# A graph network's gathers and one-hots: rolled loops with a bounds check against an unrolled program with its counts in PSUM

## The reference

```python
def _cheb_norm(src, dst, n):
    deg = jax.ops.segment_sum(jnp.ones((src.shape[0],), jnp.float32), src, num_segments=n)
    dinv = jnp.where(deg > 0, jax.lax.rsqrt(jnp.maximum(deg, 1.0)), 0.0)
    return -dinv[src] * dinv[dst]
def _cheb_conv(x, src, dst, norm, W0, W1, b):
    def prop(h):
        return jax.ops.segment_sum(h[src] * norm[:, None], dst, num_segments=x.shape[0])
    return x @ W0 + prop(x) @ W1 + b
h = _cheb_conv(x, src, dst, norm, W1_0, W1_1, b1)
h = _layer_norm(h, gamma, beta)
h = jnp.where(h >= 0, h, 0.01 * h)
out = _cheb_conv(h, src, dst, norm, W2_0, W2_1, b2)
return _layernorm(x + out)
```

## Time and profile before

| | |
|---|---|
| median of 3 runs | 2444.04 us (2441.0 to 2445.28) |
| span of the profiled execution | 3370.7 us |
| TensorE, VectorE, POOL, ScalarE busy | 61%, 46%, 50%, 15% of that span |
| first gather, last gather | 201.3 us, 3333.2 us |

### The profile page before, as it was taken

How to read it: one execution, slowest core, us unless ns; L and a number is a source line. 1 busy time by engine, 2 the same in 40 slices (tenths; PEclk the granted TensorE clock), 3 DMA queues, 4 the chain that set the end, 5 groups by cost and what they waited for, 6 DMA issues and landing times.

```text
span 3370.7 us, 41016 instructions
## 1 busy us (share of the span) xinstructions
PE 2065.1 (61%) x7250; PEld 963.6 (29%) x7251; DVE 1544.4 (46%) x3507; ACT 505.3 (15%) x1030; POOL 1700.9 (50%) x1725
## 2 busy tenths in 40 slices
PE   6836576665665665665764656565565656555655
PEld 5712232222222322232331222222222222222222
DVE  6754444444444444544443444444444434444444
ACT  5920111111111211111230000000000000000000
POOL 0156554545555554655526545554545445554543
PEclk6558887887887878887876878787777777878778
DMA  6376565655555555655646555565555555555554
GB/s 215 133 259 181 150 174 155 173 159 160 164 167 168 159 165 157 181 159 167 182 132 200 166 158 171 166 177 155 167 159 164 155 158 165 161 165 162 159 159 122
DMA packets 215109, 559.98 MB, mean 166 GB/s; under 512 B 48100, under 2 KB 49760, under 8 KB 214948
## 3 DMA queue, kind: packets, MB, share of 16 engines
q0 software_dynamic: 133120, 436.31, 45.9%
q10 hardware_dynamic: 44676, 81.73, 7.2%
q1 hardware_dynamic: 37152, 40.21, 3.6%
HBM read 493.08 MB, written 64.18 MB: 165 GB/s over the span
## 4 chain that ended last, share of the span: by engine, by line
PE 30%; another core or an unknown queue 26%; issue 25%; DVE 8%; ACT 5%; DVEq 3%; ACTq 1%; DMA 1%; POOL 1%; SPq 0%; POOLq 0%
PE bank L749 16%; PE bank L710 10%; DVE acc L947 6%; PE bank L668 2%; ACT work L556 2%; ACT feat L564 1%; DVEq L923 1%; PE bank L727 1%; PE bank L655 1%; DVEq L947 1%; DVE onehot L923 1%; POOL ring L444 1%; ACT work L546 1%; ACTq L528 0%
## 5 line engine op out<-in xcount | busy, mean ns | idle before, releaser
L444 POOL DMA_INDIRECT ring<-table,index x1664 | 1672.6, 1005 | 1466.5 <-SPq L393 952.1
L947 DVE SCALAR_TENSOR_TENSOR acc<-bank,down,acc 128x512 f32 x928 | 696.9, 751 | 1219.6 <-PE bank L710 709.8
L710 PE MATMUL bank<-ring,onehot 128*128 x3712 | 920.3, 406 | 306.0 <-issue 148.1
L749 PE MATMUL bank<-wA,feat 128*128 128x512 f32 x784 | 547.6, 863 | 804.2 <-ACT feat L564 748.2
L923 DVE TENSOR_SCALAR onehot<-count_h,dst_c,neg_tile 128x128 f16<-128x128 f16 x1856 | 489.2, 329 | 490.1 <-issue 487.6
L710 PEld LDWEIGHTS bank<-ring,onehot 128*128 128x128 f16 x3712 | 380.6, 103 | 865.6 <-issue 515.3
L749 PEld LDWEIGHTS bank<-wA,feat 128*128 128x128 f32 x784 | 212.0, 285 | 1084.9 <-ACT feat L564 774.3
L727 PE MATMUL bank<-wB,base_in 128*128 128x512 f32 x784 | 353.6, 594 | 0.0
L546 ACT ACTIVATE work<-acc 128x512 f32 (+1 forms) x98 | 61.7, 630 | 1747.4 <-issue 1039.3
L727 PEld LDWEIGHTS bank<-wB,base_in 128*128 128x128 f32 x784 | 149.5, 191 | 155.8 <-issue 142.1
L564 ACT ACTIVATE feat<-bank 128x512 f32<-128x512 f32 x98 | 58.5, 597 | 845.4 <-remote 828.7
(11 more groups left out here) (118 smaller groups left out, 689.6 us busy)
## 6 DMA issues: line engine op xcount, KB each, us to landing
ring<-table,index POOLq DMA_INDIRECT x1664
base_in<-feat ACTq DMA_DIRECT2D x98, 256.0 KB
feat<-feat SPq DMA_DIRECT2D x49, 256.0 KB, 2.9
table<-work SPq DMA_DIRECT2D x49, 256.0 KB, 3.1
feat<-feat ACTq DMA_DIRECT2D x49, 256.0 KB
table<-work ACTq DMA_DIRECT2D x49, 256.0 KB
feat<-in_x ACTq DMA_DIRECT2D x48, 256.0 KB
out<-work ACTq DMA_DIRECT2D x48, 256.0 KB
```

The costliest lines, as they stand in the source:

```text
L444: nc.gpsimd.indirect_dma_start(out=ring[:, at * ROW:(at + 1) * ROW], out_offset=None, in_=table[l], in_offset=bass.IndirectOffsetOnAxis(ap ...
L710: last = nc.tensor.matmul(bank[u % SUM_BANKS][:, :], onehot[:, u, j, :], ring[:, bass.ds(at, D)], start=j + half == 0, stop=j + half == GROUP)
L749: last = nc.tensor.matmul(to[:, :], feat[:, 2 + tile_slot, c * P:(c + 1) * P], wA[:, c * D:(c + 1) * D], start=False, stop=c == KB - 1)
L947: nc.vector.scalar_tensor_tensor(tile_of(acc, tile[u]), bank[u % SUM_BANKS][:, :], col(down[:, l, :], tile[u]), tile_of(acc, tile[u]), ALU ...
```

## The change

The program is written out: every gather, step and visit is an instruction of its own, and only the numbers that depend on the data are still loaded (four steps' at a time). Beside that:

- The gathers have no bounds check, and read their indices from one table of the whole pass. SyncE's index copies are gone.
- One instruction of VectorE makes the one-hots of four steps (line 926 of the new kernel). It compares a row of counts, fp32 in PSUM bank 3 (`count_p`), with `rel`, an fp16 table of `dst` less the tile's first node, one entry for each step and chunk. `rel` is made in setup: VectorE writes 14 `pick` matrices (line 890), TensorE multiplies them with the edges' `dst` (`pick_part`, line 625, one in each of visits 34 to 47), VectorE adds `neg_tile`.
- VectorE's sums are plain additions; the scale `down` goes into an identity that ScalarE makes for each tile (`scaled_identity`), and TensorE turns and scales the sums with it (line 736). There are three banks for sums.
- Layer norm's statistics and normalising in pass 0 read the product's PSUM bank. A visit does the dense products of the tile before (`LAG_SUMS`); the drain has 3 visits. Visits lie evenly, at `place(v)`, and VectorE's part 5 steps later.
- In setup, VectorE's tables for the walk stand between the low rows 0 to 7 and 8 to 48.

```diff
-    UNROLL = 8
-    STEP_BLOCKS = STEPS // UNROLL
-    GATHER_BLOCKS = GROUPS // UNROLL
-    RING = UNROLL
-    FREE_LAG = 4
-    SUM_BANKS = 4
+    GATHERS = GROUPS * GROUP
+    HALF = STEPS // 2
+    HALF_COLS = HALF * GROUP
...
+    HOTS = BLOCK * GROUP
+    RING = 16 // GROUP
+    FREE_LAG = RING // 2
+    USED = 8
...
+    SUM_BANKS = 3
...
-    LAG_STATS, LAG_NORMAL, LAG_HIDDEN, LAG_LEAKY, LAG_BACK, LAG_LOW = 1, 2, 3, 4, 5, 6
...
+    SPACING = STEPS * 256 // TILES
+    FIRST_PLACE = -(-STEPS // TILES) + 8 // GROUP
+    STATS_LATER = -(-STEPS // TILES) // 2
+    LAG_SUMS, LAG_NORMAL, LAG_HIDDEN = 1, 2, 3
...
+        def place(v):
+            return min(STEPS, FIRST_PLACE + (v * SPACING >> 8))
...
-            bound = pool.snap(pool.to_reg(N - 1))
             for l in range(2):
-                for slot in range(len(s_table[l])):
-                    pool.wait_ge(s_table[l][slot], 16 * uses(slot, len(s_table[l])))
-                def gathers(it, l=l):
-                    pool.wait_ge(index_in[it.slot], 16 * (GATHER_BLOCKS // 2 * l + it.turn + 1))
-                    pool.sem_inc(gathers_begun, 1)
-                    for k in range(UNROLL):
-                        wait(pool, ring_free, GROUPS * l + it.n * UNROLL + k - RING + 1)
-                        pool.sem_inc(gathers_begun, 1)
-                        for j in range(GROUP):
-                            at = k * GROUP + j
-                            nc.gpsimd.indirect_dma_start(
-                                out=ring[:, at * ROW:(at + 1) * ROW], out_offset=None, in_=table[l],
-                                in_offset=bass.IndirectOffsetOnAxis(ap=index[:, it.slot, at:at + 1], axis=0),
-                                bounds_check=bound, oob_is_err=False).then_inc(ring_landed[k], 16)
-                straight(gathers, 0, 2, 2)
-                looped(pool, gathers, 2, GATHER_BLOCKS, 2)
+                tables = (s_table0, s_table1)[l]
+                for slot in range(len(tables)):
+                    pool.wait_ge(tables[slot], 16 * uses(slot, len(tables)))
+                for g in range(GROUPS):
+                    k = g % RING
+                    wait(pool, ring_free, GROUPS * l + g - RING + 1)
+                    for j in range(GROUP):
+                        at = k * GROUP + j
+                        c = g * GROUP + j
+                        nc.gpsimd.indirect_dma_start(
+                            out=ring[:, at * ROW:(at + 1) * ROW], out_offset=None, in_=table[l],
+                            in_offset=bass.IndirectOffsetOnAxis(ap=index[:, c:c + 1], axis=0)
+                        ).then_inc(ring_landed[k], 16)
...
+            act.wait_ge(picked, 1)
+            act.dma_start(as_blocks(wA), weights(w1_1)).then_inc(s_wA[0], 16)
...
+            def scaled_identity(l, k):
+                wait(act, sums_turned, TILES * l + k - 1 if k > 1 else 0)
+                nc.scalar.activation(diag[:, k % 2, :], ident[:, :], ACT.Copy, scale=down[:, l, k:k + 1]
+                                     ).then_inc(diag_ready, 1)
...
+            def pick_part(m):
+                half, b = m // EDGE_BLOCKS, m % EDGE_BLOCKS
+                at = slice(half * HALF, (half + 1) * HALF)
+                return nc.tensor.matmul(pick_banks[half][:, 0:HALF_COLS].rearrange("p (n j) -> p n j", j=GROUP),
+                                        edge_f[1][:, b * P:(b + 1) * P], pick[b][:, at, :],
+                                        start=b == 0, stop=b == EDGE_BLOCKS - 1)
...
+                if PICK_VISIT <= it.least < PICK_VISIT + 2 * EDGE_BLOCKS:
+                    pe.wait_ge(pick_ready, 1)
+                    last = pick_part(it.least - PICK_VISIT)
+                    if it.least == PICK_VISIT + 2 * EDGE_BLOCKS - 1:
+                        last.then_inc(picked, 1)
...
+                    for c in range(KB):
+                        last = nc.tensor.matmul(bank[TURN_BANK][:, c * P:(c + 1) * P],
+                                                acc[:, bass.ds(it.n * D + c * P, P)], diag[:, it.slot, :],
+                                                start=True, stop=True)
+                    last.then_inc(sums_turned, 1)
...
+            straight(low_rows, 0, 8, 8)
             dve.wait_ge(walk_sum, 1)
-            link(nc.vector.tensor_scalar(neg_tile[:, :], bank[6][:, 0:WALK], -float(P), None, ALU.mult))
-            link(nc.vector.tensor_copy(tile_i[:, :], bank[6][0:1, 0:WALK]))
-            link(nc.vector.tensor_tensor(group_i[:, :], count[0:1, :], bank[6][0:1, 0:WALK], ALU.subtract))
-            link(nc.vector.tensor_scalar(slot_i[:, :], group_i[:, :], RING - 1, None, ALU.bitwise_and))
-            link(nc.vector.scalar_tensor_tensor(used_i[:, :], count[0:1, 0:GROUPS], 1.0, bank[7][0:1, 0:GROUPS],
-                                                ALU.add, ALU.add))
-            link(nc.vector.tensor_reduce(early_f[:, 0:1], bank[5][0:1, P:2 * P], axis=AX, op=ALU.max))
+            for half in range(2):
+                at = slice(half * HALF, (half + 1) * HALF)
+                nc.vector.tensor_scalar(tile_u[:, at], walk_banks[half][0:1, :], float(D), None, ALU.mult)
+                nc.vector.tensor_scalar(neg_tile[:, at], walk_banks[half], -float(P), None, ALU.mult)
+                link(nc.vector.tensor_tensor(group_f[:, at], count[:, at], walk_banks[half], ALU.subtract))
+            for b in range(EDGE_BLOCKS):
+                for j in range(GROUP):
+                    last = nc.vector.tensor_scalar(pick[b][:, :, j], group_f, (j - b * P) / GROUP, part_group[:, 0:1],
+                                                   ALU.add, ALU.is_equal)
+            last.then_inc(pick_ready, 1)
+            link(nc.vector.tensor_copy(group_i, group_f[0:1, :]))
+            link(nc.vector.tensor_scalar(slot_i, group_i, RING - 1, None, ALU.bitwise_and))
+            step_cols = step_u[:, :].rearrange("p (n e) -> p n e", e=ENTRY)
+            nc.vector.tensor_scalar(step_cols[:, :, 0], group_i, 1, None, ALU.add)
+            for k in range(OFFSETS):
+                nc.vector.tensor_scalar(step_cols[:, :, 1 + k], slot_i, GROUP * ROW, k * D, ALU.mult, ALU.add)
+            link(nc.vector.scalar_tensor_tensor(used_u[:, :], count[0:1, 0:GROUPS], 1.0, used_row, ALU.add, ALU.add))
+            link(nc.vector.tensor_copy(count_p, count[:, 0:P]))
+            link(nc.vector.tensor_reduce(early_f[:, 0:1], late_row, axis=AX, op=ALU.max))
             link(nc.vector.tensor_scalar(early_f[:, 1:2], early_f[:, 0:1], -1.0, float(TILES), ALU.mult, ALU.add))
             link(nc.vector.tensor_copy(early_i[:, :], early_f[:, 1:2]))
+            looped(dve, low_rows, 8, TILES - 1, 8)
+            straight(low_rows, TILES - 1, TILES, 8)
...
+            def hots(l, b):
+                if b >= BLOCKS:
+                    return
+                g = BLOCKS * l + b
+                if b >= 2:
+                    dve.wait_ge(steps_done[l], (b - 1) * BLOCK)
+                elif l:
+                    dve.wait_ge(steps_done[0], STEPS)
+                nc.vector.tensor_tensor(onehot[:, b % 2, :, :], count_p.unsqueeze(1).to_broadcast([P, HOTS, P]),
+                                        rel[:, b * HOTS:(b + 1) * HOTS].unsqueeze(2).to_broadcast([P, HOTS, P]),
+                                        ALU.is_equal).then_inc(onehots_ready, 1)
...
-                    for j in range(GROUP):
-                        last = nc.vector.tensor_scalar(onehot[:, slot, j, :], count_h[:, :],
-                                                       col(dst_c, group * GROUP + j), col(neg_tile, n),
-                                                       ALU.subtract, ALU.is_equal)
-                    last.then_inc(onehots_ready, 1)
...
-                        nc.vector.scalar_tensor_tensor(tile_of(acc, tile[u]), bank[u % SUM_BANKS][:, :],
-                                                       col(down[:, l, :], tile[u]), tile_of(acc, tile[u]),
-                                                       ALU.mult, ALU.add).then_inc(sums_added, 1)
...
+                    nc.vector.tensor_tensor(acc_at, acc_at, bank[g % SUM_BANKS][:, :], ALU.add).then_inc(sums_added, 1)
```

686 lines of the change are left out of this document (351 added, 335 removed).

## The result

| | before | after |
|---|---|---|
| median, beside each other | 2444.18 us (2441.0 to 2445.28, 4 runs) | 3109.29 us (3101.57 to 3110.77, 4 runs) |
| ratio, 95% interval | | 1.272, 1.2702 to 1.2738 |
| span of the profiled execution | 3370.7 us | 3107.5 us (its own time 3109.39) |

The change costs 665 us. The forecast was 2465, range 2180 to 2490: wrong, and outside its range.

What follows compares the result with a forecast made beforehand. POOL's gathers, 1.305 us from start to start, were taken to bound both passes, with setup, gap and tail. Before's 2444 + 15 (setup) - 1 (gap) + 7 (tail) = 2465 us; range 2180 to 2490.

Steps and rivals of the forecast that it cites:

- The part on the loops of gathers: 1664 gathers in a row on POOL, without registers, the index wait and SyncE's 104 index transfers: worth 0.
- Rival C: In the passes TensorE binds if its clock ratio falls below 0.80; at 0.75, 2548 us; chance 0.12.
- The bound of before: Runs before are bound by POOL's 1.305 us from gather to gather through both passes, and by setup, gap and tail.
- The interval: Start to start of POOL's gathers without the bounds check: kept at 1.305 us, the largest unknown.
- Rival B: Gathers on POOL get cheaper without the bounds check: 1.155 us from start to start, 2216 us; chance 0.40.
- VectorE's savings: Wider one-hots save VectorE 100 to 200 us, sums without a scale 56 us, all beside the gathers: worth 0.
- The banks: Three banks for four steps' sums on TensorE: a sum must be added within 5.2 us and takes 0.7; worth 0.
- The port: Moving the one-hots' counts out of SBUF is worth 0 to the gathers, which ran no slower beside one-hots.
- Setup: Before the first gather, VectorE's walk tables come earlier and TensorE adds picks: +15 us, bounds 5 and 20.
- Gap: Between the passes, tile 47's dense part adds 7.7 us and a shorter drain saves 8.4: -1, bounds -8 and +8.
- tail: +7: After the last steps, the dense part of the tile before is added with no saving: +7 us, bounds 0 and +10.
- 12 us lie outside the span: Build-up of before's runs from its profile sums to 2432 us; the remaining 12 us were put outside the profiled span.

Runs made afterwards that it cites:

- fast kernel: Changed kernel with two numbers a step for five and TensorE's, VectorE's and SyncE's tables in int32: 2405.38 us beside 2442.04 of before, ratio 0.985.

## Why the prediction was wrong, and where it was right

**The step that failed: the program's numbers, costed at nothing.** The part on the loops of gathers counts what the change takes away from POOL and SyncE and says "worth 0". What the same change puts on TensorE, 20 uint16 numbers a load for 8 int32 ones, is no term of the sum at all. TensorE had been named as the near engine, "129 us short of binding in pass 0", and nothing was laid on it. The two rows of before's trace that stand above (0.86 and 0.59 us, 116 times each, 169 us) were there to be read. They would have given a wrong price too, for 20 numbers of another type, but a term with a bound. In its place the runs showed 232 loads of 4.73 us, which make TensorE the bound: 664 us, gone when only their type is changed. The Trainium skill, "Runtime: NRT & Kernel Launch", "Instruction fetch mechanics", gives about 200 ns for each register loaded at launch from HBM. By that a load of 20 would be 4 us, an estimate, if loads from SBUF took the same; the row says 4.73 for uint16 and 1.36 for int32, so it fits the one type and not the other.

What the loads add can be estimated with the forecast's own figures: TensorE's work at full clock was put at 872 us for pass 0 and 817 for pass 1, and a pass has 116 loads.

| load | us a load | pass 0: 872 + 116 loads | pass 1: 817 + 116 loads | runs |
|---|---|---|---|---|
| 20 uint16 | 4.73 | 1421 | 1366 | 1423, 1362 (bound by TensorE) |
| 20 int32 | 1.36 | 1030 | 975 | 1106, 1042 |
| 8 int32 | 0.59 | 940 | 885 | 1061, 1039 (bound by gathers) |

The second row shows how rough this sum is: the kernel with 20 int32 numbers takes 1106 us in pass 0 (212.8 to 1318.9 in its trace), not 1030, and its gathers wait for the ring for 137.7 us in all, so TensorE still binds in part of that pass. The agreement of the first row is luck: TensorE was not idle for 549 us of pass 0 but for 415, since matmuls issued ahead run on beside a load, and was busy for 1008 and not for 872, at a granted clock of 0.83. The two nearly cancel. The gathers as the next bound explain why loads that are 4.14 us shorter, 960 us in all, give 704: the gathers take over after 1421 - 1039 = 382 and 1366 - 1039 = 327.

**Rival C, the other way, had the engine and not the mechanism.** "TensorE binds" came true, with 2548 us as its price. Its condition was that TensorE's work at full clock falls below 0.80 of its busy time; it was 872 / 1008 = 0.87 in pass 0 and 817 / 974 = 0.84 in pass 1, so the condition was not met. The lower granted clock, 0.83 and 0.84, is a consequence here: with the same 20 numbers in int32 it is 0.95 in both passes. A rival with TensorE as the bound needed a sum over everything that its queue does, not over the clock alone.

**The bound of before: supported.** With TensorE out of the way, the time is setup, 831 intervals, gap, 831 intervals, tail, as the forecast builds it. By its terms, for the fast kernel:

| | forecast | fast kernel |
|---|---|---|
| first gather | 216.3 | 212.2 |
| pass 0 | 1084.5 | 1061.0 |
| gap | 36.6 | 54.8 |
| pass 1 | 1084.5 | 1039.3 |
| tail | 31 | 36.4 |
| outside the span | 12 | 1.8 |
| sum | 2465 | 2405.5 |

That before itself is bound so in its 2442 us rests on the sum and on this kernel; there is no trace of it at 2442 us.

**The interval.** The forecast kept 1.305 and called it the largest unknown. It is 1.25 without the check: 0.948 busy and 0.30 idle, and putting the check back gives the 0.052 busy time again. Rival B had the direction, with 0.15 for 0.055 as its size: 1662 x 0.055 = 91 us for 249. The 0.30 idle have nothing to do with the check. The time of the fast kernel with the check, beside a before at 2442, was not measured.

**VectorE's savings, worth 0: right.** One-hots take 1.216 us, within the 1.1 to 1.5 of the forecast, sums 0.688 for 0.751; neither shows in a time. **The banks: right** as far as seen: in the fast kernel TensorE waits 185.6 us for sums, beside gathers.

**The port: right for the old form, wrong for the new.** The rows of before showed narrow one-hots by a scalar operation that cost the gathers nothing, and I carried that over to a wide operation on two tensors. With both inputs in SBUF that one does hold the gathers up. The Trainium skill, "SBUF — State Buffer", "Who interferes with whom", says that two SBUF inputs contend with GpSimd's reads, and that `tensor_tensor` is such a case; the runs agree (1.24 us for 0.95, 58 us in all). The same place infers that `tensor_tensor` does not hold up the writing of DMA descriptors; a gather here, which also reads its indices from SBUF, does take longer beside it. So moving the counts to PSUM saves nothing against before, but it is what makes the new form free.

**Setup: right in sign, 12 for 15.** The first gather moves from 201.3 to 213.2. The picks are cheaper on VectorE than taken, 0.38 us each for 0.55:

```profile
153.95 5.28 DVE L890 TENSOR_SCALAR ring<-ring,part_group 128x464 f32<-128x464 f32 x14
```

**Gap: -1 against +17; tail: +7 against +12,** both from the 37.6 and 24 us that the forecast worked out for before. In the fast kernel's gap the last steps end at 1284.1 and the next gather starts at 1328.0, 43.9 us against 33.8: three visits are left, as forecast, but two of them hold a dense part (TensorE starts them at 1290.27 and 1304.54), and a visit starts 15.1 and 13.9 us after the one before it (1288.51, 1303.61, 1317.52), where the forecast counted 4.2 for a visit and a dense part once. And those last steps end 10.9 us after the last gather of the pass began, not 3.8, because the visit of tile 47, its dense part included, is issued ahead of them:

```profile
1271.37 3.60 PE L692 MATMUL bank<-wB,base_in 128*128 128x512 f32 x8
...
1275.21 3.70 PE L692 MATMUL bank<-wA,work 128*128 128x512 f32 x8
...
1279.64 4.48 PE L685 MATMUL bank<-ring,onehot 128*128 x20
```

**"12 us lie outside the span": wrong.** In every profiled execution whose time is known it is some 1.8 us above the span (3109.39 and 3107.5; 2405.52 and 2403.7). With a before of 2442.04 and 1.8 outside, the forecast's build-up of 2432 was 8 us short. And the long span of before is not the cost of recording, as the forecast took it: before takes such times in some sets without a profile too.

The account of the fast kernel against before: 91 us from the interval, less 11 of setup, 17 of gap, 12 of tail, leaves 51; measured 37. The waits on the ring that are left in pass 0, 1061 for 1039, are 22 more; the 8 us missing from the build-up of before go the other way.

**Open:** why a set of runs has before at 3365 to 3442 or at 2442, and after at 3200 or 3109 (the sets at 3365 and above ran on three chips, the two at 2442 on two others; whether that is the reason was not tested); and why in the first kind the counts in SBUF *help* (2772 for 2869 us, in ratios 0.8235 for 0.8352 and 0.8564). Neither was settled, and no verdict above rests on it.

## What to carry to other kernels

When unrolled code still takes numbers from the data, sum for each engine's queue what it loads into registers, by count and by type, as if it were compute: the queue issues nothing meanwhile. Try such tables in int32, which was 3.5 times cheaper a number here, and keep constants out of them. And once one engine is close behind the bound, the question for each edit is not what it takes from the others but what it lays on that one.

## What the runs showed of the hardware

Register loads from SBUF, the median of one, in us; all from the runs above:

| numbers | uint16 | int32 |
|---|---|---|
| 4 (VectorE) | 0.948 | 0.344 |
| 8 (TensorE) | 1.92 | 0.59 |
| 8 (SyncE) | 1.66 | 0.53 |
| 20 (TensorE) | 4.73 | 1.36 |

A 16-bit number costs some 0.24 us (4.73 / 20) and a 32-bit one some 0.07 (1.36 / 20), 3.5 times less, though it has twice the bytes. The first column's first and third rows, in after:

```profile
L1018 DVEq TENSOR_LOAD <-tile_u x232: 942/948/2796, 218.4 to 3076.3; - x116
```

```profile
L359 SPq TENSOR_LOAD <-used_u x104: 853/1656/3982, 205.9 to 3047.3; - x104
```
